# Old products in two buffers in turn, and one more pair of pixel products summed by a transfer instead of TensorE

## The reference

```
offset, mask = split(dwconv(gn(x)) @ om_w + om_b)
value        = gn(x) @ vp_w + vp_b
sampled_k    = bilinear(value, y + ky + offset_y, x + kx + offset_x)
x            = x + sum_k(mask_k * sampled_k) @ op_w
```

## Time and profile before

| | |
|---|---|
| median of 3 runs | 3805.28 us (3805.22 to 3807.43) |
| the profiled execution | 3809.51 us, its span 3807.5 us |
| PE busy | 3566.0 us, 94% of the span |
| DVE busy | 3440.4 us, 90% |
| ACT busy | 2395.1 us, 63% |
| POOL busy | 593.5 us, 16% |
| layer 0 / change-over / layer 1 | to about 3300 / 3400 / 3807 us |

### The profile page before, as it was taken

One profiled execution on the slowest core, in us unless ns is written; L12 is line 12 of the kernel. 1 busy time (PEld: TensorE's weight loads), 2 busy tenths in 40 slices (PEclk: granted clock), 3 DMA queues, 4 the chain that ended last, 5 costly groups with the idle time before them and its releaser, 6 DMA issues. The chain is left out here.

```text
span 3807.5 us, 89724 instructions
## 1 busy us (share of the span) xinstructions
PE 3566.0 (94%) x37184; PEld 2312.6 (61%) x37184; DVE 3440.4 (90%) x2659; ACT 2395.1 (63%) x4673; POOL 593.5 (16%) x444
## 2 busy tenths in 40 slices
PE   4899999999999999999999999999999999858998
PEld 2566666666666666666666666666666666623333
DVE  4899999999999899999999999999999999948876
ACT  5676666666776667667666667667766665235554
POOL 0011111110111111111111110111111111104444
PEclk9999999999999999999999999999999999979999
DMA  7455566555655566556655655656655554345553
GB/s 175 115 126 113 125 135 144 121 119 126 140 129 115 125 141 135 106 115 140 135 119 123 141 128 121 128 130 132 135 122 118 115 110 93 58 160 212 210 214 145
DMA packets 324548, 503.88 MB, mean 132 GB/s; under 512 B 37756, under 2 KB 243196, under 8 KB 314248
## 3 DMA queue, kind: packets, MB, share of 16 engines
q0 software_dynamic: 98688, 229.66, 32.7%
q1 hardware_dynamic: 224584, 266.07, 23.3%
q10 hardware_dynamic: 832, 2.10, 0.1%
HBM read 262.53 MB, written 67.41 MB: 87 GB/s over the span
## 5 line engine op out<-in xcount | busy, mean ns | idle before, releaser
L1059 DVE TENSOR_TENSOR pv<-val,wsum 128x2048 f32<-128x2048 f32 x800 | 1809.9, 2287 | 43.3 <-PE ps_add L830 28.6
L830 PEld LDWEIGHTS ps_add<-ident,pv 128*128 128x128 f32 x12288 | 1342.7, 142 | 317.3 <-issue 163.2
L830 PE MATMUL ps_add<-ident,pv 128*128 128x128 f32 x12288 | 1456.7, 275 | 46.2 <-DVE pv L1059 44.7
L782 PE MATMUL ps_om<-xdw,omw 128*32 128x256 f32 x13824 | 867.9, 384 | 69.9 <-ACT hat L604 68.9
L1009 DVE TENSOR_TENSOR prod<-hat,mwy 128x1536 f32<-128x1536 f32 (+1 forms) x384 | 526.3, 1399 | 122.6 <-DMA wsum<-prod 98.4
L782 PEld LDWEIGHTS ps_om<-xdw,omw 128*32 128x32 f32 x13824 | 391.3, 109 | 378.7 <-ACT hat L604 91.8
L479 POOL DMA_DIRECT2D wsum<-prod x192 | 226.2, 1253 | 2255.8 <-DVE wsum L1009 2255.8
L602 ACT ACTIVATE hat<-ps_om,omb 128x256 f32<-128x256 f32 x576 | 275.0, 477 | 452.8 <-PE ps_om L782 437.8
L606 ACT ACTIVATE msk<-ps_om,omb 128x256 f32<-128x256 f32 x288 | 136.5, 474 | 365.4 <-PE ps_om L782 360.2
L753 PE MATMUL ps_bg<-tri,diag 128*32 128x512 f32 x3024 | 346.6, 592 | 12.0 <-ACT tri L568 12.0
L557 ACT ACTIVATE tri<-tri,gn_tri 96x1024 f32<-96x1024 f32 (+1 forms) x376 | 329.8, 950 | 4.7 <-ACT gn_tri L525 4.4
(11 more groups left out here) (145 smaller groups left out, 2703.7 us busy)
## 6 DMA issues: line engine op xcount, KB each, us to landing
wsum<-prod POOLq DMA_DIRECT2D x160, 768.0 KB, 6.8
tri<-in_x_dram SPq DMA_DIRECT2D x725, 128.0 KB, 2.8
win<-in_x_dram SPq DMA_DIRECT2D x144, 256.0 KB, 3.3
pv<-pv POOLq DMA_DIRECT2D x32, 1024.0 KB, 7.6
x<-xres SPq DMA_DIRECT2D x128, 256.0 KB, 5.5
xres<-in_x_dram POOLq DMA_DIRECT2D x124, 256.0 KB, 9.6
out_dram<-c_x SPq DMA_DIRECT2D x31, 1024.0 KB, 4.8
c_x<-x SPq DMA_DIRECT2D x30, 1024.0 KB, 5.3
```

Source lines behind the costliest of these rows:

```text
L782: mm = nc.tensor.matmul(ps_om[G * q:G * q + G, (par + i) % 2, 0:TOK], omw[:, h, comp, :], xdw[:, j % 2, h, q, :], start=h == 0, stop=h == ...
L830: mm = nc.tensor.matmul(ps_add[:, tb, c, :], pv[:, (j + uv) % PBUF, c, P * tb:P * tb + P], consts["ident"][:, :], start=uv == ADDED[0] and ...
L1059: nc.vector.tensor_tensor(pv[:, (j + uv) % PBUF, :, :].rearrange("p c (r w) -> p c r w", w=W), val[:, :, SR * j + u:SR * j + u + SR, v:v + ...
```

## The change

Four things change together. (1) `PAIRED` gets 3: 2, so product 2 is added into product 3 by a transfer and PE makes 23 sums a step; the new transfer stands in POOL's queue behind `load_ahead` of `acc` and ahead of tap 6's. Shift 3 is summed at k = 6 behind the early sum of 4; at k = 5 only shift 1 is left, with no early sum. (2) Old products of taps 1 and 3, and in steps j = 2 and 3 of taps 6 and 8, go to `acc` (`ahead[0]`), the others to `prod`. `products(k)` now waits for the last user of its own buffer. (3) The adding by DVE at taps 4, 5 and 8 waits for the transfers of the sent taps before it. (4) `summed` on ACT waits until the transfers of taps 1 to 3 have landed, as it overwrites `acc`.

```
-PAIRED = {1: 0}
+PAIRED = {1: 0, 3: 2}
-ADDS_AT = [..., (), (2, 1, 3), (4, 5, 6), (7, 8, 9), (10, 11, 12)]
+ADDS_AT = [..., (), (1,), (4, 3, 5, 6), (7, 8, 9), (10, 11, 12)]
+NO_AHEAD = (2, 3)
+def in_acc(j, k):
+    return k in ((1, 3, 6, 8) if j in NO_AHEAD else (1, 3))
...
 # POOL, before tap 6
     add_pair(n, j, 1)
     if j < CH and n < NI - 1:
         load_ahead(n, j, 0, "back3")
+    add_pair(n, j, 3)
...
 # ACT
 if k == BACK_AT and not first:
+    act.wait_ge(wsum_added, 16 * (sent_before(TAPS) * s + sent_before(4)))
     summed(s - 1)
...
 # DVE, products(k)
-if k > 0 and k - 1 in SENT_TAPS:
-    dve.wait_ge(wsum_added, 16 * (sent_before(TAPS) * s + sent_before(k)))
-elif k > 1:
-    dve.wait_ge(wadd_done, (TAPS - 1 - len(SENT_TAPS)) * s + kept_before(k))
+same = [i for i in range(1, k) if in_acc(j, i) == in_acc(j, k)]
+if k == 1:
+    if not is_step(n, j, 0, 0) and not is_step(n, j, 0, 1):
+        dve.wait_ge(bg_free, unit(*previous(n, j), "back3", NI) + 1)
+    if j in (1, 2) and has_next(n):
+        dve.wait_ge(sums_made, CH * CH * n + CH * j - 1)
+elif k == 6 and in_acc(j, k):
+    dve.wait_ge(bg_free, unit(n, j, "back3", NI) + 1)
+elif k > 1 and same and same[-1] in SENT_TAPS:
+    dve.wait_ge(wsum_added, 16 * (sent_before(TAPS) * s + sent_before(same[-1] + 1)))
+elif k > 1 and same:
+    dve.wait_ge(wadd_done, (TAPS - 1 - len(SENT_TAPS)) * s + kept_before(same[-1] + 1))
+elif k > 1:
+    at_least(dve, wadd_done, (TAPS - 1 - len(SENT_TAPS)) * s)
...
 # DVE, add_products(k) for k = 4, 5, 8
+dve.wait_ge(wsum_added, 16 * (sent_before(TAPS) * s + sent_before(k)))
```

More of the change, by code:

```diff
@@ L39 @@
 SAMPLED = 4
-PAIRED = {1: 0}
+PAIRED = {1: 0, 3: 2}
 PAIRS = list(PAIRED)
-ADDS_AT = [(13, 14, 15), (16, 17, 18), (19, 20, 21), (22, 23, 24), (), (2, 1, 3), (4, 5, 6), (7, 8, 9), (10, 11, 12)]
+ADDS_AT = [(13, 14, 15), (16, 17, 18), (19, 20, 21), (22, 23, 24), (), (1,), (4, 3, 5, 6), (7, 8, 9), (10, 11, 12)]
 ADDED = [uv for k in (4, 5, 6, 7, 8, 0, 1, 2, 3) for uv in ADDS_AT[k]]
@@ L337, in window_edge, with in_prod @@
             return max(0, -lo), WR - max(0, lo + WR - H)
-        def in_prod(rect):
+        def in_acc(j, k):
+            return k in ((1, 3, 6, 8) if j in NO_AHEAD else (1, 3))
+        def in_prod(rect, j, k):
             a, b, c, d = rect
             at = 6 * TOK if a == 2 and d - c == 2 else 0
-            return prod[:, at:at + (b - a) * (d - c) * TOK].rearrange("p (a b t) -> p a b t", a=b - a, b=d - c)
+            return (ahead[0] if in_acc(j, k) else prod)[:, at:at + (b - a) * (d - c) * TOK].rearrange("p (a b t) -> p a b t", a=b - a, b=d - c)
         with nc.Block() as block:
@@ L478, in add_products @@
                     for a, b, c, d in tap_rects(ky, kx)[1]:
-                        nc.gpsimd.dma_start(wsum[:, ky + a:ky + b, kx + c:kx + d, :], in_prod((a, b, c, d)), accum_op=ALU.add)\
+                        nc.gpsimd.dma_start(wsum[:, ky + a:ky + b, kx + c:kx + d, :], in_prod((a, b, c, d), j, k), accum_op=ALU.add)\
                             .then_inc(wsum_added, 16)
@@ L1013, in products @@
                     dve.wait_ge(mwy_done, TAPS * s + k + 1)
-                    if k > 0 and k - 1 in SENT_TAPS:
-                        dve.wait_ge(wsum_added, 16 * (sent_before(TAPS) * s + sent_before(k)))
+                    same = [i for i in range(1, k) if in_acc(j, i) == in_acc(j, k)]
[10 more added lines that the diff above has]
+                        dve.wait_ge(wadd_done, (TAPS - 1 - len(SENT_TAPS)) * s + kept_before(same[-1] + 1))
                     elif k > 1:
-                        dve.wait_ge(wadd_done, (TAPS - 1 - len(SENT_TAPS)) * s + kept_before(k))
+                        at_least(dve, wadd_done, (TAPS - 1 - len(SENT_TAPS)) * s)
                     at_least(dve, pv_full, SHIFTS * (s - 1) + (13, 14, 15, 18, 19, 20, 23, 24, 25)[k])
                     for rect in old:
-                        product(in_prod(rect), rect)
+                        product(in_prod(rect, j, k), rect)
                     for a, b, c, d in new:
@@ L1034, in add_products @@
                         return
+                    dve.wait_ge(wsum_added, 16 * (sent_before(TAPS) * s + sent_before(k)))
                     for a, b, c, d in tap_rects(ky, kx)[1]:
                         w = wsum[:, ky + a:ky + b, kx + c:kx + d, :]
-                        ins = nc.vector.tensor_tensor(w, w, in_prod((a, b, c, d)), ALU.add)
+                        ins = nc.vector.tensor_tensor(w, w, in_prod((a, b, c, d), j, k), ALU.add)
                     ins.then_inc(wadd_done, 1)
```

## The result

The changed kernel takes 3781.85 us (median of 4 runs, 3780.08 to 3783.27); the kernel before took 3806.36 beside it (4 runs, 3805.22 to 3811.92). The ratio is 0.9932, with a 95% interval of 0.9915 to 0.9950. The forecast was 3755, its range 3732 to 3798: faster, as said, and inside the range, but 0.68% instead of 1.3%.

The account below looks back on a forecast made before the run. PE was taken to bound layer 0, with DVE close behind. Gains of 0, 1.3, 3.4 and 1.45 us in steps 0 to 3 make 6.2 an image, 50 over 8 images: 3805.3 - 50 = 3755 us, range 3732 to 3798.

Parts of the forecast that it names:

- What bounds the kernel: Layer 0's steps: PE idle only 3.1 us a step; DVE's 3.8 us of transfer waits mostly slack, costing PE 0.8.
- A sum less on PE: Each step: 16 matmuls of 118 ns fewer on PE, saving 1.89 us.
- the early sum of tap 5: Tap 5, between second and third offset product: without it PE waits 0.4 us for ACT, net saving 1.45 a step.
- The pair's transfer and the buffers: Multiply 6 at tap 6: pair lands 7.6 us after issue, DVE waits 0.2 us (bounds 0 to 3), PE never.
- The second sign of being wrong: Tap 4: a new wait of ACT for transfers showing at k = 4 would refute the prediction.
- The transfer behind it: Tap 6's transfer, queued behind the pair's: lands 9.3 us after issue instead of 6.4, delaying tap 7's products in steps 0, 1.
- Sum over an image: Steps 0 to 3 gain 0, 1.3, 3.4 and 1.45 us: together 6.2 us an image, 50 us over 8 images.
- The mis-sized term: PE's waits for late products: 1.4 us at tap 0 of step 1, 0.7 at tap 0 of step 2; step 2's own vanish.
- Step 0 gaining as much as step 3: Sign that the prediction is wrong, since it had step 0 gaining nothing and step 3 1.45 us.
- The check by floors: Mean step: PE's floor 99.3 us, DVE's 98.8; the forecast's 100.1 a step lies 0.8 above the higher.
- dearer transfers: Tap 6's transfer in steps 0 and 1 lands some 3 us later still: 3790 us (3772 to 3803), chance 0.20.
- Free transfers: Queued transfers overlap, tap 6's lands in time, each step gains 2.25 us: 3732 us, chance 0.13.

## Why the prediction was half right

*What bounds the kernel.* Right: PE, and DVE's 3.8 us of waits for transfers were mostly slack. When they went, no more than PE's own 0.8 us a step came back: 24.1 us, where 32 x 0.8 is 25.6.

*A sum less on PE, 1.89 us, and the early sum of tap 5, 0.4 us back.* Right: the wait for ACT appears at tap 5 with 0.46 us, and the stretch from step 3 to 0 fell by 1.36 us.

*The pair's transfer and the buffers.* Right for the pair: 1.7 us of waiting for it in 2500. The second sign of being wrong, a new wait of ACT for the transfers at k = 4, didn't come either. Not foreseen: DVE waits up to 3.5 us at tap 6 and 3.0 at tap 7 of steps 3 and 0 for PE's sums 1 and 3, as PE is behind there with the projections. The kernel with the pair in steps 0, 2 and 3 keeps these waits and is faster, so most of them are slack.

*The transfer behind it.* Right in size: in steps 0 to 2 tap 6's lands 8.5 to 9.9 us after issue (once 10.5) where 9.3 was forecast and 6.4 to 7.7 was before (once 8.5); in step 3, where nobody waits for it, it lands after 10.4 to 11.4 instead of 8.0 to 9.1. Wrong in its parts: the load of the next image was given a share and has none, as step 1's is issued 6.5 us ahead of the pair and step 0's, whose bytes were counted as flowing until 7.2 us after issue, lands after 5.4 in the image shown. So the delay of 1.5 us forecast for tap 7 of step 0 came in only three of seven images, as waits of 0.5 to 1.1 us, and tap 8 of step 0, which was to keep its wait, has none: DVE now stands 1.9 to 3.0 us for PE at tap 7 before it. The 0.1 us forecast for tap 7 of step 1 is 1.4 to 3.0.

*Sum over an image.* This is the step that failed. It gave 6.2 us; the image shown gained 4.8, the mean of seven 4.0, the whole launch 28 in eight images (profiled spans), and the first two images gave only 3.8: PE's turn in the third image's step 0 begins at 926.5 us where it began at 930.2. The mis-sized term is what PE loses by waiting for late products. The prediction left 1.4 us of it at tap 0 of step 1 and 0.7 at tap 0 of step 2, and let those inside step 2 vanish, some 0.6 us a step in all; it measured 1.1, which makes up some 2 of the 2.2 us missing in an image. It also stands elsewhere: nothing at tap 0 of step 1 and 0.9 us at tap 1, and 3.4 us from tap 8 of step 1 to tap 1 of step 2. So by steps the sum is wrong in three of four: 0, 1.3, 3.4 and 1.45 us were forecast for steps 0 to 3, and 1.9, a loss of 0.5, 2.6 and 0.3 were measured. Step 0 gaining as much as step 3 was named as a sign of being wrong, and it came. Tap 7's products of step 1 were set against their old place, "just where they stand now", and so found to cost 0.1 us; but DVE comes to tap 7 sooner now, meets a wait of 1.90 there and tap 8's of 1.88 behind it, and has lost the lead that PE's shorter step calls for. Each transfer was followed, but the lead of DVE over PE was not carried from step to step. The check by floors had the same fault: it averaged DVE's waits over four steps (98.8) where step 1 alone decides. That this is the term, the kernels without the pair in step 1 show: PE's waits fall to 0.3 us a step and the stretch by 1.9 us in the mean. One reading was of a single case: the 1.48 us at tap 3 of step 2 occur in one image of seven, another has 0.4 there and the rest nothing; the total of PE's waits came from the long window, so the sum does not hang on it.

*The rivals.* The first, dearer transfers (3790), is nearest in time, and the measured time lies in its range (3772 to 3803), 10 us outside the forecast's own (3740 to 3772). Its mechanism, a transfer later than computed, isn't what happened. So that the time fell inside the stated range is partly luck: the range was made wide enough by a rival that didn't come true. Free transfers are refuted by the kernel with the pair behind tap 6's. The estimate of 4.4 us for 1 MB by the Trainium skill ("DMA: Bandwidth & Descriptors", "Anatomy of one DMA") doesn't hold here either: the two pairs' transfers land in 7.3 us in the median of 64.

*The sum over the buffers.* The sum adds only 3.7 us over the buffers in the whole launch, when the image shown has 1.8 and eight of them would be 14. The turns say where the rest went: the seven images gain 1.3 us each, 9.0 in all, but the changed kernel comes to tap 4 of the first image's step 2 2.4 us later than the kernel with the buffers alone, and needs 2.5 us more from tap 4 of the last image's step 2 to the end of the turns. Why the first and the last steps lose is left open.

## What to carry to other kernels

Where two engines in order are both some 95% busy, price a saving stretch by stretch, cut at events of the engine that bounds: work taken off pays only where the other engine's lead lasts, and a saving can be applied in some steps and left out in the one without slack, which here was better than applying it everywhere. Cut more than one stretch of each kind: the image first looked at was not the mean one. A transfer that replaces engine work delays those queued behind it by what is left of its data time when they are issued, so look at who waits for the next one in the queue. A wait that is set by ACT's order is not filled by moving PE's work into it; in three steps of four here it reappeared at the next bank, in one piece, and brought the clock down.

## What the runs showed of the hardware

Adding transfers on POOL's queue are served in order, at about 187 GB/s. 768 KB lands 6.4 us after issue at the least when nothing is ahead of it, and 8.5 to 9.9 us (steps 0 to 2, once 10.5) behind a 1 MB one issued 2.5 us before. 1 MB issued 0.7 us behind 768 KB lands after 10.7 to 14.1 us. In the kernel with the value unit moved, 20 of 23 waits of 2.10 us in PE's work were followed by about 3 us at half clock, at some 1.6 us each from steps 0 and 2; waits of 1.05 us there and of 1.26 us in the changed kernel were not.
